# Attention row sums: first additions without copies, and nine instead of ten pairs summed by TensorE

## The reference, cut to what matters

```
q, k = l2norm_axis1(q), l2norm_axis1(k)
sim = jnp.einsum('bihd,bjhd->bhij', q, k) * SCALE
attn = jax.nn.softmax(sim, axis=-1)
out = jnp.einsum('bhij,bjhd->bhid', attn, v)
```

## Time and profile before

| what | value |
|---|---|
| median of 3 runs | 5574.15 us (5572.2 to 5580.3) |
| the profiled execution | 5571.39 us, of which the span from first to last instruction is 5569.7 us |
| busy share: VectorE, TensorE, ScalarE, GpSimd | 88%, 85%, 71%, 29% |
| mean granted TensorE clock | 0.947 of full speed |
| attention stage, each batch | 531.6 us |

### The profile page before, as it was taken

One profiled execution on the slowest core, in us unless ns is written; L12 is line 12 of the kernel. 1 busy time (PEld: TensorE's weight loads), 2 busy tenths in 40 slices (PEclk: granted clock), 3 DMA queues, 4 the chain that ended last, 5 costly groups with the idle time before them and its releaser, 6 DMA issues. The chain is left out here.

```text
span 5569.7 us, 100509 instructions
## 1 busy us (share of the span) xinstructions
PE 4759.2 (85%) x34096; PEld 1989.2 (36%) x34168; DVE 4895.4 (88%) x6312; ACT 3967.8 (71%) x5761; POOL 1610.1 (29%) x790
## 2 busy tenths in 40 slices
PE   5788879998778887999867887799986788789998
PEld 2333333334333333333433333333343333333334
DVE  6799779998779977999878997799986899779998
ACT  3787569994378757999347774799934878479992
POOL 1388600000048860000004886000000488500000
PEclk9999989999889998999988999899998999999998
DMA  1000030000000003000000000300000000030000
GB/s 41 0 1 0 16 66 10 9 5 24 24 0 1 0 16 66 10 9 5 23 24 0 1 0 16 66 10 9 6 23 24 0 1 0 16 66 10 9 5 16
DMA packets 41496, 87.21 MB, mean 16 GB/s; under 512 B 11531, under 2 KB 27734, under 8 KB 37974
## 3 DMA queue, kind: packets, MB, share of 16 engines
q1 hardware_dynamic: 41046, 81.11, 5.5%
HBM read 26.55 MB, written 8.39 MB: 6 GB/s over the span
## 5 line engine op out<-in xcount | busy, mean ns | idle before, releaser
L1553 ACT ACTIVATE arena<-ps 128x1024 f32<-128x1024 f32 x2048 | 1912.3, 1035 | 187.3 <-PE ps L1516 176.6
L1582 DVE TENSOR_TENSOR arena<-arena 128x1024 f32<-128x1024 f32 x1664 | 1900.8, 1225 | 25.1 <-ACT arena L1553 25.1
L1165 DVE TENSOR_TENSOR_SCAN arena<-ps,hlast,arena 128x512 f32<-128x512 f32 x1024 | 1253.8, 1271 | 26.0 <-ACT hlast L1047 11.6
L1110 POOL TENSOR_TENSOR arena<-arena 128x1024 f32<-128x1024 f32 x512 | 1201.1, 2355 | 239.9 <-ACT arena L1026 173.3
L1516 PE MATMUL ps<-arena 128*32 128x512 f16 x16384 | 1089.0, 381 | 113.5 <-issue 82.3
L1499 PE MATMUL ps<-arena 128*32 128x512 f32 x8192 | 1065.8, 598 | 7.2 <-ACT arena L1553 3.6
L932 PE MATMUL ps<-arena,ident 128*128 128x512 f32 x2048 | 965.6, 596 | 6.1 <-ACT arena L1026 5.2
L1044 ACT ACTIVATE ps<-arena,amat 128x512 f32<-128x512 f32 x1024 | 704.5, 688 | 354.7 <-DVE arena L1165 345.7
L1516 PEld LDWEIGHTS ps<-arena 128*32 128x32 f16 x16384 | 464.1, 97 | 965.0 <-issue 666.9
L1883 POOL MEMSET arena<- 128x1024 f32 x4 | 3.8, 951 | 2447.0 <-POOLq L103 2447.0
L1141 DVE TENSOR_TENSOR arena<-arena,ps 128x1024 f32<-128x1024 f32 x416 | 499.6, 1201 | 75.2 <-remote 51.8
(11 more groups left out here) (278 smaller groups left out, 4501.0 us busy)
## 6 DMA issues: line engine op xcount, KB each, us to landing
arena<-x SPq DMA_DIRECT2D x32, 512.0 KB, 5.5
arena<-arena SPq DMA_DIRECT2D x64, 256.0 KB, 6.0
arena<-arena SPq DMA_DIRECT2D x64, 224.0 KB, 5.9
arena<-arena SPq DMA_DIRECT2D x28, 512.0 KB, 3.8
arena<-pe SPq DMA_DIRECT2D x256, 32.0 KB, 1.8
out<-arena SPq DMA_DIRECT2D x8, 1024.0 KB, 4.3
expw<-L_ffn_expert_w SPq DMA_DIRECT2D x1, 512.0 KB
wqkv<-L_attn_W_qkv SPq DMA_DIRECT2D x1, 192.0 KB
```

Of the source, the lines that this page charges most:

```text
L1110: pool.tensor_tensor(halves(hb[s % RING]), halves(hb[s % RING]), cs[s % 4].unsqueeze(1).broadcast_to([128, HD, CH]), ALU.mult).then_inc(hc ...
L1165: dve.tensor_tensor_scan(halves(hb[s % RING])[:, h, :], da(s, h), halves(injected)[:, h, :], k.hlast[:, s, h, :], ALU.mult, ALU.add).then_ ...
L1553: act.activation(probs[p % 8], k.bank(2 * group[p], 2 * CH), ACT.Exp, scale=SCALE / SPLIT ** 2).then_inc(exp_s, 1)
L1582: dve.tensor_tensor(acc[p % 2], acc[p % 2], probs[p % 8], ALU.add).then_inc(acc_s, 1)
```

## The change

The pairs that TensorE sums directly are now listed as pairs and not as blocks. They are those of the blocks 5, 11, 17, 23 and 29, but for pair 59 (the second of block 29), which VectorE adds now: nine pairs. At block 29 TensorE sums pair 58 alone, heads 0 and 1. VectorE's first addition of an accumulator takes two pairs from their buffers, 0 and 2 for the even one and 1 and 3 for the odd one, in place of a copy of pair 0 or 1 and an addition of pair 2 or 3. VectorE thus issues 53 instructions for the sum in each chunk in place of 54. The counts that the waits use (`summed`) follow from that: buffers 0 and 1 come free with the additions of pairs 2 and 3, and an addition waits for the one before it on the same accumulator.

```diff
--- before.py
+++ after.py
@@ -1468,8 +1468,9 @@
 
     group = [p % 3 for p in range(NPAIR - 1)] + [1]
 
-    direct = [j for j in range(NJ) if j % 6 == 5]
-    NA = NPAIR - 2 * len(direct)
+    direct = [p for p in range(NPAIR) if p // 2 % 6 == 5 and p != NPAIR - 5]
+    by_vector = [p for p in range(2, NPAIR) if p not in direct]
+    NA = len(by_vector)
 
     def first(c):
         return isinstance(c, int) and c == 0
@@ -1477,24 +1478,26 @@
     def summed(c, p):
 
 
-        before, p = (0, p + NPAIR) if p < 0 else (NA, p)
-        return c * NA + (before + sum(i // 2 not in direct for i in range(p + 1)))
+        before, p = (0, p + NPAIR) if p < 0 else (NA, p + 2 if p < 2 else p)
+        return c * NA + (before + sum(i <= p for i in by_vector))
 
     def tensor(pe):
-        def ones_by(t, start, stop):
-            for h in range(HEADS):
+        def ones_by(a, t, start, stop):
+            for h in (2 * a, 2 * a + 1):
                 last = pe.matmul(k.ps[32 * h:32 * h + 32, LS * CH:(LS + 1) * CH], k.ones[:, 0:32],
-                                 t[h // 2][:, (h % 2) * CH:(h % 2 + 1) * CH], start=start, stop=stop, tile_position=(0, 32 * h))
+                                 t[:, (h % 2) * CH:(h % 2 + 1) * CH], start=start, stop=stop, tile_position=(0, 32 * h))
             return last
 
         def weigh(c, j):
             pe.wait_ge(exp_s, c * NPAIR + (2 * j + 2 + 3))
             if j == 0 and not first(c):
                 pe.wait_ge(o_s, c)
-            if j == direct[0] and not first(c):
-                pe.wait_ge(l_s, c)
-            if j in direct:
-                ones_by([probs[(2 * j + a) % 8] for a in range(2)], j == direct[0], False)
+            for a in range(2):
+                p = 2 * j + a
+                if p == direct[0] and not first(c):
+                    pe.wait_ge(l_s, c)
+                if p in direct:
+                    ones_by(a, probs[p % 8], p == direct[a], False)
             for h in range(HEADS):
                 last = pe.matmul(k.ps[32 * h:32 * h + 32, O * CH:(O + 1) * CH], v[:, j * 128 + 32 * h:j * 128 + 32 * h + 32],
                                  probs[(2 * j + h // 2) % 8][:, (h % 2) * CH:(h % 2 + 1) * CH],
@@ -1503,7 +1506,8 @@
 
         def finish(c, q):
             pe.wait_ge(acc_s, summed(c, NPAIR - 1))
-            ones_by(sums[q], False, True).then_inc(l_mm, 1)
+            ones_by(0, sums[q][0], False, True)
+            ones_by(1, sums[q][1], False, True).then_inc(l_mm, 1)
 
         def body(c, q, queries):
             for j in range(NJ):
@@ -1572,13 +1576,13 @@
         def body(c, q):
             acc = sums[q]
             for p in range(NPAIR):
-                if p // 2 in direct:
+                if p not in by_vector:
                     continue
                 dve.wait_ge(exp_s, c * NPAIR + (p + 1 + 3))
-                if p < 2:
-                    dve.tensor_copy(acc[p % 2], probs[p % 8]).then_inc(acc_s, 1)
+                if p < 4:
+                    dve.tensor_tensor(acc[p % 2], probs[p - 2], probs[p], ALU.add).then_inc(acc_s, 1)
                 else:
-                    dve.wait_ge(acc_s, summed(c, p) - 2)
+                    dve.wait_ge(acc_s, summed(c, max(i for i in by_vector if i < p and i % 2 == p % 2)))
                     dve.tensor_tensor(acc[p % 2], acc[p % 2], probs[p % 8], ALU.add).then_inc(acc_s, 1)
                 if p == 5 and not first(c):
                     divide(c - 1)
```

## The result

The changed kernel's median is 5583.54 us over 20 runs (5574.51 to 5592.6), that of the kernel before 5575.11 over 20 runs; the ratio is 1.0016, 95% interval 1.001 to 1.0022. That is 8.4 us slower (the interval is 5.6 to 12.3), under the 11 us that the prediction took as its line, though the upper end of the interval lies above it. 5583.54 is inside the range of 5556 to 5586 and just past the narrower 5576 to 5583 that the prediction gave for its own account; the loss is 3.6 us more than its forecast of 4.8. The prediction had said that a measurement couldn't tell so little from no change. With 20 runs it could: the interval leaves out 1. Two later comparisons gave 1.0016 again (1.0007 to 1.0025 both times).

What follows compares the result with a forecast made beforehand. The attention stage was taken as paced by TensorE at direct blocks and ScalarE between them. Terms 0 + 4.8 + 0 gave +4.8 us, so 5579.0 us; own range 5576 to 5583, 8-in-10 range 5556 to 5586.

Steps and rivals of the forecast that it cites:

- the 11 us that the prediction took as its line: Whole kernel's time: a difference under 0.2% (11 us) was to count as no change.
- The copies are worth nothing: Chunk start on VectorE: removing two copies gains 0, as pair 2's addition waits for its exponential; 1.2 us without that cover.
- TensorE saves nothing with two heads less: Block 29 on TensorE: summing pair 58 alone saves 0, since array parts 0 and 1 still do 0.86 us of ones.
- Nothing is lost at 28 chunk ends: Usual chunk ends: TensorE's closing sum comes 0.33 us late, its 0.52 us wait for ScalarE takes that up; worth 0.
- The four ends cost 4.8 us: Each batch's last chunk: last addition, closing sum, reciprocal and block end come 1.21 us later; 4.8 us slower in all.
- The sum, 4.8 against 8.4 measured: Whole kernel: the terms 0 + 4.8 + 0 make it 4.8 us slower, 5579.0 us.
- Half the sum, half the time: Rival, block 29 on TensorE: two parts take one step, 0.43 us less in 28 chunks; -7.2 us, 5567; chance 0.08.
- The free parts let the next work through: Rival, block 29: free array parts run ahead, ScalarE is released 0.86 us earlier; -17.2 us, 5557; chance 0.18.
- The late closing sum reaches ScalarE: Rival, usual chunk ends: TensorE's lateness passes its 0.52 us cover, up to 0.33 in 20 ends; +11.4 us, 5586; chance 0.06.
- The uneven block costs a step: Rival, block 29: heads 0 and 1 hold up heads 2 and 3, 0.43 us more; +16.8 us, 5591; chance 0.06.
- VectorE's spare time as a bound for each chunk: Chunk starts: VectorE has about 0.8 us to spare a chunk; one rival's gain was capped at 0.755 in 20 chunk ends.

Runs made afterwards that it cites:

- e3: Changed kernel's copies part alone (no copies, TensorE still sums all ten pairs), against the kernel before: ratio 1.0008.
- e4: Pair 59's part alone: copies kept, VectorE adds pair 59, TensorE sums nine pairs, against the kernel before: ratio 1.0021.
- e6: Changed kernel with pairs 11, 23, 35 and 47 left out of the sum, VectorE's work unchanged: ratio 1.0013 to the kernel before.
- e7: Changed kernel with pair 58 summed by nobody, so block 29 has no ones matmul: ratio 0.9998 to the kernel before.
- e5: Changed kernel, but in each batch's last chunk TensorE keeps pair 59: ratio 0.9996 to the kernel before, median 5571.06 us.
- e9: Kernel before with another batch end: TensorE sums pairs 62 and 63, sums come ahead of the last weighing: ratio 0.9985, 5569.43 us.
- e11: Changed kernel with a new batch end: TensorE sums pairs 62 and 63, ahead of the last weighing: ratio 0.9999 to the kernel before.
- e8: TensorE sums four whole blocks (6, 13, 20, 27), VectorE adds 54 pairs without copies: ratio 1.0035 to the kernel before.
- e1: The changed kernel run again without any edit, against the kernel before: ratio 1.0016.
- e12: The changed kernel run a third time, with one more profile, against the kernel before: ratio 1.0016.

## Why the prediction was right, point by point

- *The copies are worth nothing.* Right as it was meant, for the copies alone: pair 2's addition waits for its exponential in the changed kernel too (0.39 us), and e3 without copies is not faster. Beside pair 59 they are worth something, which the prediction had only for a chunk whose cover is gone: with the copies kept (e4) the closing sum waits 2.7 us for VectorE at a batch's end, without them 1.7.
- *TensorE saves nothing with two heads less.* Right, shown three times: two steps at 1089.15 and 1089.61 in the profile after, the 0.75 us of ScalarE unchanged, and e6. That a block does cost its 0.8 us, and that this is on the path, e7 shows.
- *Nothing is lost at 28 chunk ends.* Right: the chunks without a turn agree to 0.02 us where the clock stayed up, and e5 keeps them all and loses nothing. The eight ends with a turn scatter too much to be compared one by one; they show no loss. The lateness of the closing sum, 0.33 in the prediction, was taken up by TensorE's wait, which shrank by 0.26.
- *The four ends cost 4.8 us.* Right in place and mechanism, a little small in size. The term was 1.21 us a batch; it measured 4.98 - 3.69 = 1.29, or 5.2 us in all. Most of the difference is the dependent step from pair 57 to 59. It was taken as 1.26 from the reciprocal and its product; in the loop's chunks the starts lie 1.25 apart, in the last chunk (and in chunk 0) 1.32. e5 gave the whole loss back.
- *The sum, 4.8 against 8.4 measured.* 5.2 is shown in the chunks. One of 12 profiled ends of the changed kernel paid 0.88 us more for a fallen clock, which the prediction had not seen: its longer wait exposes TensorE to that. Over a whole execution this is 0.3 us. What is left of the 8.4, some 3 us, I can't place: the forecast was low by it, and its cause stays open. The profiled executions differ among themselves by more than that (turns with a fallen clock, and stages outside attention); it came back in three comparisons, so chance alone is an unlikely answer, but no run here isolates it. It is not a toll on every variant: e5 lies 2 to 5 us below its account, e9 1 to 2, and e11, with all of the changed kernel's chunks, is even with the kernel before. The two runs that made the late end shorter (e5, e11) gave back some 10 us against the changed kernel, where the profiled ends account for 5.2 and 5.6. That points at the end of a batch and away from the chunks, but with intervals of 5 us to each side it isn't shown.
- *Half the sum, half the time.* Refuted by e6.
- *The free parts let the next work through.* The first half is true and visible, the second is not. The parts without ones work do start the next weighing 0.86 and the next scores 0.82 us ahead. ScalarE was nevertheless released only when the slow parts were through: the semaphore's update came 0.86 us after the end of the record of the matmul that carries it.
- *The late closing sum reaches ScalarE.* It didn't. The step in the loop's chunks was 1.25, and TensorE's wait of 0.52 covered it.
- *The uneven block costs a step.* Refuted: the columns 1>2 and 6>7 are unchanged, 65.09 and 65.15 us beside 65.10 and 65.16.
- *VectorE's spare time as a bound for each chunk.* This stood under the rivals' prices and was wrong; no term of the forecast used it. e4 needs 0.45 us more than is spare at a chunk's start, and no chunk got longer; e4 and e8 show that the debt is paid at the end.

## What to carry to other kernels

Work that is split over parts of TensorE's array cost here what its busiest part costs: taking two of four heads away from a step took nothing off it, so whole steps have to go, and only where the engine that takes the work over has room (e8 took a whole block away and was 19 us slower). A consumer behind a ring of buffers needn't bound each round; as long as the ring holds its debt, the debt is read at the end of the stage, where nothing follows that hides it. So an engine's last work there should be made short first, as e9 did. Look also for the neighbours that an edit makes dependent: leaving one pair out of an alternating sequence put two additions to one accumulator behind each other.

## What the runs showed of the hardware

- The four 32-column parts of TensorE work at their own pace. With the ones matmuls of two parts missing, the others took up later instructions in the same step, 0.03 us behind (1089.15 and 1089.18). The signal of the scores hangs on the last matmul, on a part that was 0.8 us ahead; it was given at 1091.53, after the slow parts' earlier matmuls of the same pair, and ScalarE's exponential came as late as before. So the signal kept the program's order where the work did not. The Trainium skill, TensorEngine Tiling (Array Packing), section Tiling Modes, says that different tiles can load weights and multiply in parallel. The trace agrees (1089.15 and 1089.18); of the order of the signals the page says nothing.
- An addition of 128 x 1024 float32 took a step of 1.135 us when the one before it was on the other accumulator, and 1.25 to 1.32 when it depended on it.
- Behind waits for VectorE TensorE's clock was found at 1.2 GHz in some places and not in others, and a closing sum that met it took 1.37 to 1.94 us instead of 1.06. Behind waits of 1.70 to 1.73 us this came at 1 of 16 batch ends (the first profile, e1, e6, e12), behind waits of 2.0 to 3.7 us at 11 of 12 (e4, e7, e8). The same wait in the same program (1.71 and 1.72 us in two profiles) met both. A loop turn with a fallen clock cost 0.7 to 1.5 us more.
